# One down-projection for two expert slots, with the sum formed on GpSimd, in two of eight expert blocks

## The reference

```
logits = xn @ Wg.T                     # 8 experts
(v0, e0), (v1, e1) = the two largest   # K = 2 slots
g0, g1 = softmax(v0, v1)               # g1 / g0 = exp(v1 - v0)
h_i = silu(W1 xn + B1[e_i] A1[e_i] xn) * (W3 xn + B3[e_i] A3[e_i] xn)      # 896 wide, i = 0, 1
x = x + sum_i g_i * (W2 h_i + B2[e_i] (A2[e_i] h_i))
```

## Time and profile before

| | us |
|---|---|
| median of three runs | 1312.70 |
| the profiled execution's own time | 1312.18 |
| its span, first to last instruction | 1310.4 |
| TensorE busy (matmuls) | 1202.5 |
| VectorE busy | 677.2 |
| ScalarE busy | 416.9 |
| GpSimd busy | 229.6 |

### The profile page before, as it was taken

The page is one execution under the profiler, slowest core; times in us unless marked ns, Lnnn a source line. Parts: engine busy times, 40 slices in busy tenths (PEclk is TensorE's granted clock), DMA queues, the critical chain, the costliest instruction groups (busy, mean ns, idle before and its releaser), DMA issues.

```text
span 1310.4 us, 17604 instructions
## 1 busy us (share of the span) xinstructions
PE 1202.5 (92%) x6865; PEld 916.2 (70%) x6865; DVE 677.2 (52%) x1661; ACT 416.9 (32%) x897; POOL 229.6 (18%) x133
## 2 busy tenths in 40 slices
PE   6889999999998989988787999999999989899888
PEld 5677675767866778667565776757678677786666
DVE  5753266664465456334634433666644655663351
ACT  3623021313222342433453431313133223424352
POOL 0000074560110210000000000836501102100000
PEclk9999999999999999989998999999999999998989
DMA  8200000000000000000000000000000000000000
GB/s 350 115 1 1 1 1 1 1 1 1 1 1 2 1 1 1 1 2 9 1 9 1 1 1 1 1 0 1 0 1 1 1 1 1 1 1 2 1 1 17
DMA packets 3570, 17.32 MB, mean 13 GB/s; under 512 B 288, under 2 KB 2464, under 8 KB 2976
## 3 DMA queue, kind: packets, MB, share of 16 engines
q1 hardware_dynamic: 2912, 14.12, 2.7%
q10 hardware_dynamic: 576, 2.08, 0.4%
HBM read 15.15 MB, written 1.05 MB: 12 GB/s over the span
## 4 chain that ended last, share of the span: by engine, by line
PE 70%; DVE 11%; issue 9%; ACT 6%; POOL 2%; DMA 0%; DVEq 0%; POOLq 0%; ACTq 0%
PE bank L684 66%; ACT scr L1278 3%; PE bank L701 2%; DVE XnT L1960 2%; DVE XnT L1962 1%; DVE scr L1552 1%; DVE stat L1544 1%; POOL rstd L2116 1%; DVE negmax L1634 1%; PE bank L802 1%; DVE X L1537 1%; PE bank L1089 1%; ACT scr L1256 1%; POOL fac L2116 1%; ACT XnT L1256 1%
## 5 line engine op out<-in xcount | busy, mean ns | idle before, releaser
L684 PE MATMUL bank<-pack,scr 128*128 128x512 f32 (+2 forms) x944 | 312.1, 483 | 8.5 <-ACT scr L1256 7.5
L684 PE MATMUL bank<-XnT,pack 128*128 128x256 f32 x1024 | 251.3, 385 | 11.9 <-ACT XnT L1256 7.1
L684 PEld LDWEIGHTS bank<-pack,scr 128*128 128x128 f32 x944 | 178.5, 193 | 114.9 <-issue 89.4
L684 PE MATMUL bank<-scr,pack 128*128 128x256 f32 x944 | 227.0, 380 | 1.3 <-DVE scr L1715 1.1
L684 PEld LDWEIGHTS bank<-XnT,pack 128*128 128x128 f32 x1024 | 191.7, 192 | 45.4 <-ACT XnT L1256 9.6
L684 PEld LDWEIGHTS bank<-scr,pack 128*128 128x128 f32 x944 | 178.1, 190 | 30.3 <-issue 4.4
L2138 POOL TENSOR_TENSOR scr<-scr 128x1024 f32<-128x1024 f32 x64 | 149.9, 2379 | 47.3 <-DVEq L1777 46.6
L2116 POOL TENSOR_TENSOR rstd<-veps,half 128x2 f32<-128x2 f32 x32 | 22.3, 698 | 750.2 <-DVE veps L1549 750.2
L1725 DVE TENSOR_TENSOR scr<-bank,scr 128x256 f32<-128x256 f32 x112 | 47.2, 423 | 149.5 <-ACT scr L1329 148.6
L1278 ACT ACTIVATE scr<-bank,negmax 128x256 f32<-128x256 f32 (+1 forms) x256 | 82.9, 445 | 92.5 <-DVE negmax L1634 92.5
L1329 ACT ACTIVATE scr<-bank 128x256 f32<-128x256 f32 x112 | 42.6, 384 | 210.5 <-PE bank L684 210.3
(11 more groups left out here) (178 smaller groups left out, 1384.9 us busy)
## 6 DMA issues: line engine op xcount, KB each, us to landing
pack<-pack_dram SPq DMA_DIRECT2D x1, 6152.0 KB, 17.5
pack<-pack_dram SPq DMA_DIRECT2D x1, 2180.0 KB, 29.6
pack<-pack_dram SPq DMA_DIRECT2D x1, 1595.0 KB, 23.5
X<-x SPq DMA_DIRECT2D x4, 256.0 KB, 16.9
pack<-pack_dram SPq DMA_DIRECT2D x1, 1024.0 KB, 20.3
pack<-pack_dram ACTq DMA_DIRECT2D x1, 975.5 KB, 6.3
pack<-pack_dram SPq DMA_DIRECT2D x1, 793.5 KB, 25.0
out_dram<-X SPq DMA_DIRECT2D x3, 256.0 KB, 2.1
```

The costliest lines, as they stand in the source:

```text
L684: return pe.matmul(o, l, r, start=start, stop=stop, skip_group_check=True)
```

## The change

In blocks with k = 0 and s even (`joined`: block a and block c):

- VectorE spreads r over 128 columns (`ratio_rows`), TensorE turns it by multiplying with the identity (`ratio`, 4 records of 128 columns, one more PSUM bank), ScalarE copies it to `ratio_t`, the place of `aT[s][:, 2]`, which by then is read.
- After each product of the second slot GpSimd does h_1 = h_1 * r and h_1 = h_1 + h_0 in place, 128x256 each, and signals `sum_ready`.
- `down` of slot 0 multiplies with columns 256 to 511 alone; `down` of slot 1 works on the sum with all 512, and waits for `sum_ready`.
- VectorE leaves out the two additions to X of slot 0. The gated one-hots change: slot 0 gets g0 (onehot_0 - onehot_1), slot 1 g0 onehot_1, so that A2 of the sum and of h_0 combine to what was there before.

```
+            JOINED: k == 0 and s % 2 == 0
 lanes:      (halves, s even)
+                return range(3, 8) if name == "ratio" else range(0, 3)
 experts:
             for m in range(FT + 2):
+                if m == 0 and joined(k, s):
+                    stage("ratio_rows", k, s)
                 if m < FT and (m or (k == 0 and s % 2 == 0)):
                     stage("x_first", k, (s, m))
+                if m == 1 and joined(k, s):
+                    stage("ratio", k, s)
                 others(f"f{m}")
 TensorE:
+            def ratio(k, s):
+                pe.wait_ge(ratio_ready[s], nth_sum(k, s, 1, 1))
+                o = claim(pe, ("ratio", (k, s)))
+                for a in range(NT):
+                    last = mm(o[:, a * P:(a + 1) * P], ratio_w[s][:, a, :], ident, True)
+                last.then_inc(full[ring.bank(("ratio", (k, s)))], 1)
 down:
                     if i == 1 and a == 0:
                         wait_drained(pe, ("x", r, m))
-                    last = mm(o[:, :], x2T[s][:, i, m, a * P:(a + 1) * P], wd[:, m, :], m == 0, m == FT - 1)
+                    if i == 1 and a == 0 and joined(k, s):
+                        pe.wait_ge(sum_ready[s], nth_sum(k, s, FT, m + 1))
+                    c0 = D if i == 0 and joined(k, s) else 0
+                    last = mm(o[:, c0:2 * D], x2T[s][:, i, m, a * P:(a + 1) * P], wd[:, m, c0:2 * D],
+                              m == 0, m == FT - 1)
 ScalarE:
+            def ratio(k, s):
+                key = ("ratio", (k, s))
+                wait_full(act, key)
+                move(key, ratio_t[s], psum(key, T))
 VectorE, gates (behind the three instructions that make g0 and g1):
+                if joined(k, s):
+                    link(dve.tensor_tensor(onehotw[s][:, :, 0, :], onehot[s][:, :, 0, :], onehot[s][:, :, 1, :],
+                                           ALU.subtract))
+                    for a in range(NT):
+                        step(dve.tensor_scalar(onehotw[s][:, a, 0, :], onehotw[s][:, a, 0, :], rw[s][:, 0, a:a + 1],
+                                               None, ALU.mult))
+                        step(dve.tensor_scalar(onehotw[s][:, a, 1, :], onehot[s][:, a, 1, :], rw[s][:, 0, a:a + 1],
+                                               None, ALU.mult))
+                    settle()
+                    return
+            def ratio_rows(k, s):
+                dve.wait_ge(top_exp[s], nth(s, 2, k + 1))
+                dve.tensor_copy(ratio_w[s], rw[s][:, 2, :].unsqueeze(2).broadcast_to([P, NT, P]))\
+                   .then_inc(ratio_ready[s], 1)
 down:
-                link(dve.scalar_tensor_tensor(out=X[s][:, a, :], in0=o[:, 0, :], ...
+                if i or not joined(k, s):
+                    link(dve.scalar_tensor_tensor(out=X[s][:, a, :], in0=o[:, 0, :], ...
 GpSimd:
+            def x_second(k, sm):
+                s, m = sm
+                if not joined(k, s):
+                    return
+                if m == 0:
+                    wait_drained(pool, ("ratio", (k, s)))
+                pool.wait_ge(x2_first[s], nth(s, 2 * FT, k * FT + m + 1))
+                wait_drained(pool, ("x", (k, s), m))
+                x2 = x2T[s][:, 1, m, :]
+                pool.tensor_tensor(x2, x2, ratio_t[s], ALU.mult).then_inc(scaled[s], 1)
+                pool.wait_ge(scaled[s], nth_sum(k, s, FT, m + 1))
+                pool.tensor_tensor(x2, x2, x2T[s][:, 0, m, :], ALU.add).then_inc(sum_ready[s], 1)
```

More of the change, by code:

```diff
@@ L307, in hybrid_kernel @@
         am_ready = each("am_ready")
+        ratio_ready = each("ratio_ready")
+        scaled = each("scaled")
+        sum_ready = each("sum_ready")
         silu_ready = each("silu_ready")
@@ L410, in hybrid_kernel, with joined, nth_sum @@
         halves, weave, summing, alone, scores_first = [False], [False], [False], [False], [False]
+        def joined(k, s):
+            return k == 0 and s % 2 == 0
+        JOINED = [[k for k in range(2) if joined(k, s)] for s in range(S)]
+        def nth_sum(k, s, per, n):
+            ks = JOINED[s % S]
+            return nth(s, per * len(ks), ks.index(k) * per + n)
         def lanes(name, k, s):
@@ L1224, in ffn_half @@
                     last.then_inc(full[ring.bank(key)], 1)
-            table = dict(head_prod=nothing, spread2=nothing, delta_sq=nothing, consts=nothing, top_exp=nothing, ffn_half=ffn_half, delta_expand=nothing, delta_diag=nothing, conv_tap=nothing, gates=nothing, down_sum=down_sum, angles=nothing, norm_x=nothing, norm_t=norm_t, latent=latent, kv=kv, kv_fold=kv_fold,
+            table = dict(ratio=ratio, ratio_rows=nothing, head_prod=nothing, spread2=nothing, delta_sq=nothing, consts=nothing, top_exp=nothing, ffn_half=ffn_half, delta_expand=nothing, delta_diag=nothing, conv_tap=nothing, gates=nothing, down_sum=down_sum, angles=nothing, norm_x=nothing, norm_t=norm_t, latent=latent, kv=kv, kv_fold=kv_fold,
                          scores=scores, weights=weights, values=values, values_t=values_t, out_in=out_in, out_proj=out_proj, router=router, spread_t=spread_t, spread=spread, x_first=x_first,
@@ L1492, in angles @@
                 act.activation(expA[:, :], w("c_alog"), ACT.Exp).then_inc(trig_out, 1)
-            table = dict(head_prod=nothing, spread2=nothing, delta_sq=nothing, consts=nothing, top_exp=top_exp_, ffn_half=nothing, delta_expand=nothing, delta_diag=nothing, conv_tap=conv_tap, gates=nothing, down_sum=nothing, angles=angles, norm_x=nothing, norm_t=norm_t, latent=latent, kv=nothing, kv_fold=nothing,
+            table = dict(ratio=ratio, ratio_rows=nothing, head_prod=nothing, spread2=nothing, delta_sq=nothing, consts=nothing, top_exp=top_exp_, ffn_half=nothing, delta_expand=nothing, delta_diag=nothing, conv_tap=conv_tap, gates=nothing, down_sum=nothing, angles=angles, norm_x=nothing, norm_t=norm_t, latent=latent, kv=nothing, kv_fold=nothing,
                          scores=scores, weights=weights, values=values, values_t=nothing, out_in=out_in, out_proj=nothing, router=router, spread_t=spread_t, spread=nothing, x_first=x_first,
@@ L2092, in angles @@
                 ins.then_inc(trig_in, 1)
-            table = dict(head_prod=nothing, spread2=spread2, delta_sq=delta_sq, consts=consts, top_exp=nothing, ffn_half=nothing, delta_expand=delta_expand, delta_diag=delta_diag, conv_tap=conv_tap, gates=gates, down_sum=nothing, angles=angles, norm_x=norm_x, norm_t=nothing, latent=latent, kv=kv, kv_fold=kv_fold,
+            table = dict(ratio=nothing, ratio_rows=ratio_rows, head_prod=nothing, spread2=spread2, delta_sq=delta_sq, consts=consts, top_exp=nothing, ffn_half=nothing, delta_expand=delta_expand, delta_diag=delta_diag, conv_tap=conv_tap, gates=gates, down_sum=nothing, angles=angles, norm_x=norm_x, norm_t=nothing, latent=latent, kv=kv, kv_fold=kv_fold,
                          scores=scores, weights=weights, values=values, values_t=values_t, out_in=nothing, out_proj=out_proj, router=router, spread_t=nothing, spread=spread, x_first=x_first,
@@ L2186, in delta_o @@
                       [P, NT * GH]).then_inc(orms[s], 1)
-            table = dict(head_prod=head_prod, spread2=nothing, delta_sq=delta_sq, consts=nothing, top_exp=nothing, ffn_half=nothing, delta_expand=nothing, delta_diag=nothing, conv_tap=nothing, gates=nothing, down_sum=nothing, angles=nothing, norm_x=norm_x, norm_t=nothing, latent=nothing, kv=nothing, kv_fold=nothing,
+            table = dict(ratio=nothing, ratio_rows=nothing, head_prod=head_prod, spread2=nothing, delta_sq=delta_sq, consts=nothing, top_exp=nothing, ffn_half=nothing, delta_expand=nothing, delta_diag=nothing, conv_tap=nothing, gates=nothing, down_sum=nothing, angles=nothing, norm_x=norm_x, norm_t=nothing, latent=nothing, kv=nothing, kv_fold=nothing,
                          scores=nothing, weights=nothing, values=nothing, values_t=nothing, out_in=nothing, out_proj=nothing, router=nothing, spread_t=nothing, spread=nothing, x_first=nothing,
-                         x_second=nothing, down=nothing, lora_t=nothing, lora=nothing,
+                         x_second=x_second, down=nothing, lora_t=nothing, lora=nothing,
                          heads_in=nothing, head_scores=nothing, head_mix=nothing, head_out_t=nothing,
```

13 lines of the change are left out of this document (8 added, 5 removed).

## The result

| | before | after |
|---|---|---|
| median | 1312.27 us (6 runs, 1311.32 to 1315.37) | 1299.47 us (6 runs, 1297.35 to 1303.65) |
| the profiled execution | 1312.18 | 1299.7 |
| its span | 1310.4 | 1297.9 |
| mean granted TensorE clock | 0.983 | 0.988 |

The ratio is 0.9903, 95% interval 0.9885 to 0.992: faster by 12.8 us. The direction was right, the amount was not.

What follows compares the result with a forecast made beforehand. TensorE, busy nearly throughout both blocks at full clock, was taken as the bound. Block a -3.9 (-5.94 + 0.96 + 1.1) and block c -4.5 (-5.94 + 0.45 + 1.0) gave -8.4: median 1304.2 us, range 1300.3 to 1308.5.

Steps and rivals of the forecast that it cites:

- Records of 256 columns, -5.94 per block: In down of slot 0, 28 records take 0.217 instead of 0.429 us each: 5.94 us less in each block.
- Rival 4: In down, 256-column records take as long as 512 because of stationary loads; nothing gained, 1315; chance 0.02.
- Start of block a, +0.96: norm_t in block a starts later by subtraction 0.21, ratio_rows 0.30 and ratio 0.45: +0.96 us (0.9 to 1.1).
- GpSimd, 0.62 us per instruction, 1.3 per tile: After second-slot products, 256 elements cost 0.62 us (0.55 to 0.83), 1.3 per tile (1.15 to 1.7); sum_ready waits free.
- What is held up: Beside GpSimd, VectorE's small SBUF chains are held up, angles by 1.3 us; products, PSUM copies and residuals pass.
- Rival 2: GpSimd's block on VectorE makes TensorE late behind all 14 second-slot products: 18 us against 10.1 gained, about 1320; chance 0.05.
- `x_first` 4, +1.1: In block a, x_first 4 waits for its bank behind the held-up angles and SiLU: 1.1 us (0 to 1.5).
- Block c, -4.5: Block c sums -5.94 for down, +0.45 for ratio and +1.0 wait for the norm of d: -4.5 us.
- Rival 1: More removed work was cover: one block keeps half its 5.94, 1307.3, or both do, 1310; chance 0.13.
- rival 3: The extra bank claim in block a changes later bank waits, +-6 us over 32 attention units: 1298 or 1310; chance 0.12.
- Sum, -8.4: Whole kernel: block a -3.9 and block c -4.5 give -8.4 us, with all bounds -10.1 to -7.4.
- The sign that the prediction named for being wrong: Outside the two blocks, TensorE idle time differing by over 2 us would show the forecast wrong.

Runs made afterwards that it cites:

- four blocks: The changed kernel with two stages reordered and the same change in two more blocks (k = 1, s odd), ratio ahead of x_first: 1315.11 us, ratio 1.0014.
- block a alone: The kernel before with only block a changed, block c as before: 1309.63 and again 1309.68 us, ratios 0.9966 and 0.9971.
- block c alone: The kernel before with only block c changed, block a as before: 1304.4 and again 1304.48 us, ratios 0.9942 and 0.9945.
- TensorE is padded: The changed kernel with idle multiplications before the last down stage, 22 in block a, 20 in block c: 1313.58 and 1314.08 us, ratios 1.0005 and 1.0012.

## Why the prediction was wrong, point by point

- *Records of 256 columns, -5.94 per block:* right. 5.97 by the run of 56 records in block a. Rival 4 is out.
- *Start of block a, +0.96:* right in kind, too large: +0.62. `ratio_rows` took 0.29 (0.30 taken), `ratio` 0.55 (0.45). But the wait for VectorE grew only from 0.74 to 0.82 us. The four gated one-hots of the changed `gates` are single multiplications and pay for the linked subtraction, which I had counted alone: I costed what was added to `gates` and not what its other instructions became. ScalarE's copy ran at 89.11 us, in a gap ahead of its copy of `XnT`; the 4.24 us of the earlier trace rows that I had put it into begin only at 95.03. It cost nothing.
- *GpSimd, 0.62 us per instruction, 1.3 per tile:* 0.726 and 1.54, inside the bounds (0.55 to 0.83) and nearer to the upper. The line through the 384 and 768 rows didn't carry down to 256. The cover was far larger, as stated: TensorE waits nowhere for GpSimd in `down`.
- *What is held up:* right. The small chain in SBUF was (3.82 to 4.75 us, +0.93; forecast 1.3), the products from PSUM were not. (The rule of the Trainium skill, "SBUF — State Buffer", section "Summary: rules for kernel authors", that the second of two such instructions is blocked until the first is done, agrees with L2130 and L2134 above. It held in the other direction too: with four blocks, GpSimd's product took 1.31 instead of 0.73 us at 366.25. The 5.86 us of L1844 above go beyond the rule: it stood through three instructions of GpSimd, not one.) Rival 2 is out.
- *`x_first` 4, +1.1:* the wait is at its place, 0.44 us in the profile, 0.60 by the distance between records. It was too large because `angles` was held up by 0.93 and not by 1.3 us, and because the slack was 0.33 us where the working had 0.2. The 0.96 ahead of it cancels, since it moves both sides of the wait.
- *Block c, -4.5:* -4.35. `norm_t` waits 0.88 where 1.0 was said, and the 1.96 us forecast to arrive ahead of it were 1.94. The second `down` saves its 2.96. Rival 1 is out, and rival 3 too as far as these two profiles show: outside the blocks and before 1200 us the distance between the two executions changes only in and beside stretches of half clock.
- *Sum, -8.4:* the structural part was -9.0 by the blocks' traces and -9.3 ± 0.5 at equal half-clock time (-8.0 to -9.9 with slopes of 0.39 to 0.22). The bounds stated for the terms make -9.6 to -7.9, and not the -10.1 to -7.4 of the prediction, and the 10.1 in rival 2 is 9.5 by its terms; neither would have changed the outcome.
- **The step that failed** is the sum itself. It went over from the two blocks to the kernel's time with no term for the clock outside them, although the page of before showed a mean of 0.983, so 45 us at half clock. The mean gain of 12.4 is 4.0 more than forecast. Of these, 0.9 are structural (9.3 for 8.4) and 11.3 x 0.28 = 3.1 are less time at half clock (2.5 to 4.4 with the slopes of single kernels). The range was built from bounds of the listed costs, and so had no room for it either. The sign that the prediction named for being wrong, idle time of TensorE outside the blocks that differs by over 2 us, did come, with +2.8 us; but it is a loss, and the gain outside is 6.2 us of busy time, from work that ran at 2.4 instead of 1.2 GHz.

Shown: the surplus isn't in the blocks (traces); it belongs to the kernels and not to one execution (block a alone and block c alone, each twice, 50 and 34 us at half clock), and it goes when TensorE is padded; and one more us at half clock goes with 0.28 us. Not shown: what decides whether a stretch falls to half clock. The place in time alone does not, by the 0.4 us between block a alone and block c alone. The same wait and the same work ahead of it led to both outcomes, and two executions of the kernel before had it at different places. So the cause of the 11 us less at half clock stays open; it is a measured property of these two kernels, and only its possibility, not its size, could have been read from the profile.

## What to carry to other kernels

Where the mean granted clock of the kernel before is below 1, a change can move half-clock time in stages that it doesn't touch: put a term for it into the range, of a few us to either side here, and compare kernels at equal half-clock time before an explanation is built on the rest. Cost a stage that is edited by its old and new instructions together, not by the added ones. Before a saving is copied to a similar block, ask again what hides its preparation: the same edit gave 4.7 and 4.4 us where a tile of TensorE work covered the ratio, and cost some 4 us where the ratio came first and `down` had been the cover of another chain.

## What the hardware showed that was not expected

- GpSimd's product or sum of two full 128x256 operands in SBUF takes 0.726 us; 128x384 with a small second operand takes 0.830. The count of elements alone doesn't give the price.
- One 128x256 subtraction on VectorE, both operands in SBUF, took 5.86 us beside three products of GpSimd in one execution, and 1.24 us in another execution of the same kernel; TensorE came 4.3 us later by it.
- Executions of one kernel differ in time at half clock more than many changes are worth: means of 55 and 36 us for the same kernel in two sets of runs (4 and 6 executions, on two chips), with medians 5.4 us apart.
- A microsecond at half clock goes with 0.28 us of time here, not 0.5: TensorE's waits, 0.73 instead of 1.38 us in the same place in the two executions (the wait for VectorE at 1207.80 before and at 1199.12 after), take up a part of it.
